# A graph layer's edge sort: one row per edge, or rows of 16 edges packed by one-hot products and written by adding scatters

## The reference

```python
def head(w1, bb1, w2, bb2, a1, aab1, a2, aab2):
    feats = jnp.maximum(x @ w1 + bb1, 0.0) @ w2 + bb2        # 256 -> 256 -> 64
    x_cat = jnp.concatenate([feats[row], feats[col], elem[:, None]], axis=1)
    hid = jnp.maximum(x_cat @ a1 + aab1, 0.0)
    e1 = (hid @ a2 + aab2)[:, 0]
    e1 = jax.nn.leaky_relu(e1, negative_slope=0.2)
    w = jnp.exp(e1 - jnp.max(e1))
    pooled = jax.ops.segment_sum(w[:, None] * feats[col], row, num_segments=n)
    row_sum = jax.ops.segment_sum(w, row, num_segments=n) + 1e-10
    return pooled / row_sum[:, None]
x = _layernorm(x + transpose(vmap(head)(...)).reshape(n, -1))
```

## Time and profile before

| | |
|---|---|
| time, median of 3 runs | 6067.9 us (6063.4 to 6071.91) |
| the profiled execution's own time | 6098.69 us |
| its span | 6096.9 us |
| PE / DVE / ACT / POOL busy in the span | 4346.8 / 4243.0 / 3138.2 / 3789.0 us |
| mean granted TensorE clock | 0.866 |
| instructions in the trace | 127641 |
| indirect DMAs of POOL | 1600 scatters, 1664 gathers |

### The profile page before, as it was taken

The page is one execution under the profiler, slowest core; times in us unless marked ns, Lnnn a source line. Parts: engine busy times, 40 slices in busy tenths (PEclk is TensorE's granted clock), DMA queues, the critical chain, the costliest instruction groups (busy, mean ns, idle before and its releaser), DMA issues.

```text
span 6096.9 us, 127641 instructions
## 1 busy us (share of the span) xinstructions
PE 4346.8 (71%) x24741; PEld 3053.9 (50%) x24742; DVE 4243.0 (70%) x23832; ACT 3138.2 (51%) x10707; POOL 3789.0 (62%) x3738
## 2 busy tenths in 40 slices
PE   3645555454555546189999999999999999999940
PEld 1423333332333323066667766676676766666630
DVE  7644444444444444378888888888888888888863
ACT  0211111111111111078888888888888888888842
POOL 6878777778777877745555555555555555555532
PEclk9867777776777777599999999999999999999975
DMA  1221222222122222267777777777777777777733
GB/s 59 50 47 29 50 33 43 38 39 46 30 50 32 44 36 36 50 202 217 217 218 216 218 216 216 216 218 215 216 216 218 218 218 212 213 219 216 210 114 119
DMA packets 298498, 833.67 MB, mean 137 GB/s; under 512 B 113010, under 2 KB 152050, under 8 KB 298342
## 3 DMA queue, kind: packets, MB, share of 16 engines
q0 software_dynamic: 184320, 666.30, 42.1%
q1 hardware_dynamic: 71614, 149.77, 8.0%
q10 hardware_dynamic: 42408, 16.21, 1.0%
HBM read 733.35 MB, written 96.91 MB: 136 GB/s over the span
## 4 chain that ended last, share of the span: by engine, by line
PE 36%; POOL 31%; issue 16%; ACT 6%; DMA 4%; DVE 4%; DVEq 0%; another core or an unknown queue 0%; SPq 0%; POOLq 0%; ACTq 0%
POOL records L556 31%; PE psum L753 15%; PE psum L740 9%; PE psum L757 9%; ACT z L850 4%; DMA out_dram<-z 3%; PE psum L766 2%; DVE z L1179 2%; DMA p_win<-p_table 1%; PE psum L777 1%; ACT onehot L879 1%; DVE acc L976 1%; ACT onehot_t L868 1%; DVE z L1169 1%; DVE acc L1228 1%
## 5 line engine op out<-in xcount | busy, mean ns | idle before, releaser
L587 POOL DMA_INDIRECT z<-qf_table,rec x1664 | 1598.1, 960 | 1565.9 <-PE psum L740 926.7
L556 POOL DMA_INDIRECT records<-z x1600 | 1942.5, 1214 | 503.5 <-issue 503.5
L850 ACT ACTIVATE z<-z 128x64 f32<-128x64 f32 x6656 | 1651.2, 335 | 56.7 <-ACT z L857 28.8
L753 PE MATMUL psum<-p_win,onehot_t 128*128 x9984 | 1438.0, 277 | 235.8 <-issue 128.0
L753 PEld LDWEIGHTS psum<-p_win,onehot_t 128*128 128x128 bf16 x9984 | 965.9, 97 | 805.3 <-issue 488.5
L740 PE MATMUL psum<-z,onehot 128*128 128x260 f32 x3328 | 1027.2, 391 | 2.6 <-DVE acc L1228 1.6
L757 PE MATMUL psum<-z,ident 128*128 128x258 f32 x3328 | 1006.6, 384 | 0.0
L1179 DVE SCALAR_TENSOR_TENSOR z<-z,a_b 128x129 f32<-128x129 f32 x3328 | 888.9, 290 | 0.0
L1179 DVE SCALAR_TENSOR_TENSOR z<-psum,a_b 128x129 f32<-128x129 f32 x3328 | 820.8, 282 | 3.3 <-issue 3.3
L651 PE MATMUL psum<-z,ones_b 125*128 125x400 bf16 (+1 forms) x1600 | 344.3, 310 | 656.2 <-DVE z L968 656.1
L1169 DVE TENSOR_TENSOR z<-z,psum 128x258 f32<-128x258 f32 x1664 | 690.3, 415 | 117.3 <-PE psum L757 87.0
(11 more groups left out here) (162 smaller groups left out, 5640.7 us busy)
## 6 DMA issues: line engine op xcount, KB each, us to landing
qf_table<-acc SPq DMA_DIRECT2D x100, 378.9 KB
p_table<-acc SPq DMA_DIRECT2D x100, 377.9 KB
p_win<-p_table SPq DMA_DIRECT2D x100, 377.9 KB
z<-qf_table,rec POOLq DMA_INDIRECT x1664
records<-z POOLq DMA_INDIRECT x1600
acc<-in_x_dram SPq DMA_DIRECT2D x25, 500.0 KB
z<-in_x_dram SPq DMA_DIRECT2D x20, 625.0 KB
out_dram<-z ACTq DMA_DIRECT2D x20, 625.0 KB
```

Source lines behind the costliest of these rows:

```text
L556: pool.indirect_dma_start(out=records, out_offset=bass.IndirectOffsetOnAxis(ap=pos_at[0:EP, s, c:c + 1], axis=0), in_=rec_out[0:EP, s, 4 * ...
L587: pool.indirect_dma_start(out=z_t[:, o + j, :], out_offset=None, in_=qf_table, in_offset=bass.IndirectOffsetOnAxis(ap=rec[:, o + j, 3:4].b ...
L753: mm = pe.matmul(to, onehot_t[:, j, :], p_flat[:, bass.ds((w % 2) * (3 * ZW) + (part * ZW + o), n)], start=(part == 0), stop=(part == 2 an ...
L850: op = act.activation(z_t[:, slot, o:o + DO], z_t[:, slot, o:o + DO], ACT.Copy, scale=z_t[:, slot, o + DO:o + HF])
```

## The change

A block is now 16 edge columns (100 blocks, four to a group, 2000 edges each). The 1600 scatters of single edges become three adding scatters per block:

- The place of each edge (`pick`) comes from PE as before, but the base of each column and window is worked out for the whole kernel in setup and added by PE, so that no count is carried from step to step. Setup therefore masks and keeps the histogram of each quarter of a block (`hist_take`), turns it around, sums it and makes three tables from it.
- A place is split in a chunk (16 records) and a slot in it (`split`). DVE makes `placed`, for each edge its six bfloat16 fields in its slot of 16 (`slots`), and the one-hot of the edge's chunk among 320 (`chunks`, 16 instructions per block). PE multiplies them (`place`, 16 products per block), which gives the sum of up to 320 chunk rows of 96 numbers; ACT takes it from PSUM (`take_sum`), PE turns it and fetches the block's step table (`turn_rows`), and DVE makes the row numbers (`row_ids`).
- POOL issues three indirect DMAs per block with `compute_op=ALU.add`, of 128, 128 and 64 rows of 384 bytes, into `sorted_rows`, which SP has filled with zeros. Before each block's three POOL waits until those of the block before have landed. That is 300 in all.
- The window one-hots move from DVE to ACT, with 16 Abs and 4 Relu instructions per block (`windows`). The features leave PSUM on ACT too, with the product with `A1` (`take_q`), and PE's transposes for them become 128 more columns of that product. ACT's work gets a written order like the others'.
- The loop has 26 turns of the group, since a block passes its last step three blocks after its first.
- Behind the loop, 13 bulk steps (`BULK`) read `sorted_rows` back (384 KB each), turn each field on PE, write the records' fields on DVE and ACT, and store them to `records`. DVE clears the accumulator before them, and they wait for all scatters.

Of the diff the core stands here; left out are the buffers' places, the semaphores, the arithmetic of the setup tables (some 45 more small DVE instructions, and four over 1600 columns before POOL's lines 536 to 540, which now come after the histogram), ACT's rewritten node work, which is as before, and the rewritten window arithmetic.

```diff
     EP = 125
     EC = E // EP
-    CPI = EC // GROUPS
-    SUBS = 4
-    LOT = CPI // SUBS
+    CB = 16
+    BLOCKS = EC // CB
     CH = 4
-    CHUNKS = LOT // CH
-    assert N == WN * W and E == EP * EC and CPI * GROUPS == EC and CHUNKS * CH * SUBS == CPI
+    PER = BLOCKS // GROUPS
+    S = 16
+    NF = 6
+    SF = S * NF
+    KC_MAX = 320
+    KB = [128, 128, 64]
+    assert N == WN * W and E == EP * EC and CB * BLOCKS == EC and PER * GROUPS == BLOCKS and CB == 4 * CH
...
+    CHUNKS = NT * P // S
+    sorted_rows = nc.dram_tensor("sorted_rows", (CHUNKS + 3 * P, SF), F32, kind="Internal").ap()
...
+        def sort_loop(eng, group):
+            group(0)
+            group(1)
+            with nc.Fori(2, GROUPS - 1, engines=bass.OrderedEngineSet([eng.engine]), hint_back_edge=True) as g:
+                group(g)
+            group(GROUPS - 1)
+            group(GROUPS)
...
-            for n in range(SUBS):
-                sp.wait_ge(s_scat[n], 16 * LOT * GROUPS)
+            sp.wait_ge(s_scat, 48 * BLOCKS)
             rec_d = records.rearrange("(p t) n -> p (t n)", p=P)
+            rows_g = sorted_rows[0:CHUNKS, :].rearrange("(g t c) n -> g t (c n)", t=P, c=P // S)
+            def load_stage(g):
+                since(sp, s_field_mm, g - 1)
+                sp.dma_start(stage[:, g % 2, :], rows_g[g, :, :]).then_inc(s_stage[g % 2], 16)
+            load_stage(0)
+            for g in range(BULK):
+                if g + 1 < BULK:
+                    load_stage(g + 1)
+                sp.wait_ge(s_field_a, g + 1)
+                sp.wait_ge(s_field_b, g + 1)
+                sp.dma_start(rec_d[:, g * P * 4:(g + 1) * P * 4], rec_all[:, g * P:(g + 1) * P, :].rearrange("p t n -> p (t n)")).then_inc(s_rec_st, 16)
+            sp.wait_ge(s_rec_st, 16 * BULK)
...
             def scatter(g):
-                for s in range(SUBS):
-                    pool.wait_ge(s_at, g * 2 * SUBS + 2 * s + 2)
-                    pool.sem_inc(s_passed, 1)
-                    for c in range(LOT):
-                        pool.indirect_dma_start(
-                            out=records, out_offset=bass.IndirectOffsetOnAxis(ap=pos_at[0:EP, s, c:c + 1], axis=0),
-                            in_=rec_out[0:EP, s, 4 * c:4 * c + 4], in_offset=None, compute_op=ALU.bypass).then_inc(s_scat[s], 16)
-            loop(pool, GROUPS, scatter)
+                for b in range(PER):
+                    if live_b(g, b, -3):
+                        h = g * PER + (b - 3)
+                        pool.wait_ge(s_row_i, h + 1)
+                        since(pool, s_scat, h * 48)
+                        pool.sem_inc(s_passed, 1)
+                        for k in range(3):
+                            pool.indirect_dma_start(
+                                out=sorted_rows, out_offset=bass.IndirectOffsetOnAxis(ap=row_i[0:KB[k], (b - 3) % 2, k:k + 1], axis=0),
+                                in_=rows_out[0:KB[k], (b - 3) % 2, 2 * (W + 1) + k * SF:2 * (W + 1) + (k + 1) * SF], in_offset=None, compute_op=ALU.add).then_inc(s_scat, 16)
+            sort_loop(pool, scatter)
+            pool.wait_ge(s_sum, 4 * BLOCKS)
+            pool.iota(win_iota, [[P, NT]], base=0, channel_multiplier=0, allow_small_or_imprecise_dtypes=True).then_inc(s_win_iota, 1)
...
             def prefix(g, q):
-                n = g * (CPI // CH) + q
+                n = g * (PER * 4) + q
                 pe.wait_ge(s_oh, n + 1)
-                since(pe, s_carry, n)
-                o = psum[:, q % 2, :]
-                for c in range(CH):
-                    oh = win_oh[0:EP, q % 2, c, :]
-                    pe.matmul(o[:, (c + 1) * W:(CH + 1) * W].rearrange("p (c w) -> p c w", w=W), ones_b[0:EP, :],
-                              oh.unsqueeze(1).to_broadcast([EP, CH - c, W]), start=(c == 0), stop=False, skip_group_check=True)
-                    mm = pe.matmul(o[:, c * W:(c + 1) * W], before[0:EP, :], oh, start=False, stop=(c == CH - 1),
-                                   skip_group_check=True)
-                mm.then_inc(s_count, 1)
+                since(pe, s_pos, n - 1)
+                o = psum[:, q % 2, 0:CH * W]
+                own = ident_b[0:BLOCKS, bass.ds(g * PER + q // 4, 1)].to_broadcast([BLOCKS, P])
+                at = slice(q % 4 * CH * W, (q % 4 + 1) * CH * W)
+                pe.matmul(o, own, base_hi[0:BLOCKS, at], start=True, stop=False)
+                pe.matmul(o, own, base_lo[0:BLOCKS, at], start=False, stop=False)
+                pe.matmul(o, before[0:EP, :], win_oh[0:EP, q // 4 % 2, q % 4 * CH:(q % 4 + 1) * CH, :].rearrange("p c w -> p (c w)"),
+                          start=False, stop=True).then_inc(s_count, 1)
+            def place(g, b, j):
+                n = (g * PER + (b - 2)) * 4 + j
+                pe.wait_ge(s_chunks, n + 1)
+                if j == 0:
+                    pe.wait_ge(s_placed, g * PER + (b - 1))
+                    since(pe, s_sum_ev, g * PER + (b - 2))
+                for c in range(j * CH, (j + 1) * CH):
+                    mm = pe.matmul(psum[0:SF, 7, 0:KC_MAX], placed[0:EP, b % 2, c, :], chunk_oh[0:EP, b % 2, c, :],
+                                   start=(c == 0), stop=(c == CB - 1))
+                mm.then_inc(s_sum, 1)
+            def turn_rows(g, b):
+                h = g * PER + (b - 3)
+                pe.wait_ge(s_sum_ev, h + 1)
+                since(pe, s_row_f, h)
+                since(pe, s_f_ev, min(g * 2 + b // 2 * 2, GROUPS * 2) if isinstance(g, int) else g * 2 + b // 2 * 2)
+                for k in range(3):
+                    pe.matmul(psum[0:KB[k], 4, 2 * (W + 1) + k * SF:2 * (W + 1) + (k + 1) * SF], chunk_t[0:SF, k * P:k * P + KB[k]], ident_b[0:SF, 0:SF], start=True, stop=True)
+                own = ident_b[0:BLOCKS, bass.ds(h, 1)].to_broadcast([BLOCKS, P])
+                for u in range(3):
+                    mm = pe.matmul(psum[:, 4, 0:2 * (W + 1)], own, step_p[0:BLOCKS, u, :], start=(u == 0), stop=(u == 2))
+                mm.then_inc(s_turned, 1)
...
+            pe.wait_ge(s_sum_ev, BLOCKS)
+            for g in range(BULK):
+                pe.wait_ge(s_stage[g % 2], g // 2 * 16 + 16)
+                since(pe, s_field_a, g - 1)
+                since(pe, s_field_b, g - 1)
+                for f in range(NF):
+                    mm = pe.matmul(psum[:, g % 2 * 6 + f // 3, f % 3 * P:(f % 3 + 1) * P],
+                                   stage[:, g % 2, :].rearrange("p (s f) -> p f s", f=NF)[:, f, :], ident[:, :], start=True, stop=True)
+                mm.then_inc(s_field_mm, 1)
...
+            def windows(g, b, j):
+                n = (g * PER + b) * 4 + j
+                since(act, s_pos, n - 7)
+                for c in range(j * CH, (j + 1) * CH):
+                    op = act.activation(win_oh[0:EP, b % 2, c, :], iota_win[0:EP, 0, :], ACT.Abs, scale=-1.0,
+                                        bias=edge_win[0:EP, bass.ds((g * PER + b) * CB + c, 1)])
+                op.then_inc(s_win_dist, 1)
+                act.wait_ge(s_win_dist, n + 1)
+                own = win_oh[0:EP, b % 2, j * CH:(j + 1) * CH, :].rearrange("p c w -> p (c w)")
+                act.activation(own, own, ACT.Relu, scale=-1.0, bias=ones_f[0:EP, 0:1]).then_inc(s_oh, 1)
+            def take_sum(g, b):
+                h = g * PER + (b - 3)
+                act.wait_ge(s_sum, h * 4 + 4)
+                since(act, s_turned, h)
+                act.activation(chunk_t[0:SF, :], psum[0:SF, 7, 0:KC_MAX], ACT.Copy).then_inc(s_sum_ev, 1)
...
+            def hist_take(n, b):
+                dve.wait_ge(s_hist, n + 1)
+                dve.tensor_tensor(hist_m[:, b, :, :, :], psum[:, b, 0:HG * HCOL * LO].rearrange("p (m c n) -> p m c n", m=HG, c=HCOL),
+                                  same_col.unsqueeze(1).to_broadcast([P, HG, HCOL, LO]), ALU.mult).then_inc(s_hist_mask, 1)
+                dve.wait_ge(s_hist_mask, n + 1)
+                dve.tensor_reduce(count_m[:, bass.ds(n * HG, HG), :], hist_m[:, b, :, :, :].rearrange("p m c n -> p m n c"), AX_X, ALU.add).then_inc(s_hist_ev, 1)
...
+            def pick(g, b, j):
+                n = (g * PER + b) * 4 + j
+                since(dve, s_pos, n)
+                dve.wait_ge(s_count, n + 1)
                 for c in range(CH):
+                    op = dve.scalar_tensor_tensor(out=picked[0:EP, c, :], in0=psum[0:EP, j % 2, c * W:(c + 1) * W], scalar=1.0,
+                                                  in1=win_oh[0:EP, b % 2, j * CH + c, :], op0=ALU.mult, op1=ALU.mult,
+                                                  accum_out=place_f[0:EP, b % 2, j * CH + c:j * CH + c + 1])
                 op.then_inc(s_pos, 1)
+            def split(g, b):
+                h, r = g * PER + (b - 1), (b - 1) % 2
+                dve.wait_ge(s_pos, h * 4 + 4)
+                dve.tensor_copy(place_i[0:EP, :], place_f[0:EP, r, :]).then_inc(s_split, 1)
+                dve.wait_ge(s_split, h * 4 + 1)
```

(66 more changed lines are left out.)

599 lines of the change are left out of this document (358 added, 241 removed).

## The result

The changed kernel takes **5817.0 us** (median of 4 runs, 5811.07 to 5817.94) where the kernel before took 6067.8 beside it: a ratio of **0.9585** (95% interval 0.9568 to 0.9601), 251 us less. The forecast was 5440 us with a range up to 5790. The direction was right, the gain 40% of the 628 us expected, and the time lies 27 us outside the range.

What follows compares the result with a forecast made beforehand. The prediction took POOL's issue of scatters to bound the first stage. Setup 185, loop 1625, drain 20, tail 115 and second stage 3522 gave a span of 5467 us; the median, 0.5% under the profiled run, was forecast at 5440, range 5230 to 5790.

Steps and rivals of the forecast that it cites:

- What bounds the kernel before: First stage: bound by POOL's issue of 1600 scatters, one every 1.52 us, 97 us per group; other engines have room.
- Loop: Sort loop: 65 us a group from three engines passing work over PSUM; 1625 us for 25 groups, plus 20 draining.
- DVE, PE, ACT per group: Sort loop: work per group of 56 us for DVE, 50 for PE at full clock, 48 for ACT.
- the prediction's 0.14 us: DVE's chunk one-hot by the skill's page, four bfloat16 columns at once; the sum would be lower by up to 150 us.
- Clock: PE in the sort loop: full clock, 2.4 GHz, since it is busy some three quarters with short pauses.
- Setup: Before the loop: loop start at 185 us, 57 later than in the kernel before.
- Tail: Behind the loop: 48.6 us of DVE work, 13 bulk steps in 61, and 5 for transfers; 115 us.
- Second stage: From the end of the sort to the end of the span: 3522 us, untouched by the change.
- (a): Sort loop: PE's clock stays low or handoffs bite harder; 79 us a group, 5790 us in all; chance 0.20.
- (b): Sort loop: engines overlap fully, a group costs DVE's 56 us; 5215 us in all; chance 0.12.
- (d): Sort loop: DVE keeps POOL from issuing scatters, a block takes 26.5 us; about 6750 us in all; chance 0.03.
- (e): Whole change: it doesn't do what it says, or row scatters cost POOL far more; about no change; chance 0.01.

Runs made afterwards that it cites:

- experiment 8: e1 with the scatters writing their rows without adding (records not whole, only the time read); 5526.3 us.
- experiment 7: e1 with DVE doing the nodes' work of each step before the four chunk one-hots; 5397.2 us.
- e1: Changed kernel with SP issuing the qf_table store before the p_table store; 5535.8 us, ratio 0.9073 to the kernel before.
- experiment 6: e1 with POOL splitting the weights beside the histogram and not behind it; the loop begins at 194.9 us, in e1 at 193.3.
- experiment 5: e1 with POOL clearing the accumulator beside the bulk steps and making win_iota before the last two blocks' scatters; 5460.4 us.
- e4: Changed kernel with DVE making each chunk one-hot twice, the extra one into a spare tile; 5945.5 us.
- series A: The follow-up runs from e1 to e4, on one chip; the kernel before took 6102.4 us there.
- series B: Follow-up runs on another chip, among them experiment 5, experiment 6 and experiment 7; the kernel before took 6065.8 us there.
- series C: Experiment 8 and e10, on another chip; the kernel before took 6093.3 us there.
- e10: e1 plus the changes of experiment 5 and experiment 7, with every 125-row load and store cut in 112 and 13; 5280.1 us, ratio 0.8665.

## Why the prediction was wrong, and where it was right

- **What bounds the kernel before**: right. The scatters left the chain and were hidden by a wide margin (experiment 8).
- **Loop: the failed step.** The forecast priced the work of the engines and their handoffs over PSUM: the sum of each step's longest, 69, less slack, 65 us. It had no term for the landing of the stores that ACT now waits for. The change moved window one-hots and features to ACT, behind `take_q`, whose wait had cost little as long as the loop waited for POOL anyway. The missing term is a wait of 16.7 us a group (418.2 us in 25), of which 12.7 are paid. With the wait gone, in three different ways, a group costs 66.6 to 67.6. One resource was left out: a buffer that a store gives back. That 65 and 66.6 lie so close is in part luck: DVE's work was put some 5 us a group too high, and 4 us a group were the order that experiment 7 changes, for which the sum had no term.
- **DVE, PE, ACT per group.** Forecast 56, 50 and 48 us. From the window of e1 (busy share times 66.6): DVE 1106.08 / 1450 gives 50.8, PE 54.7 at a clock of 0.93, ACT 43.6. ACT's 43.6 is 4 below its forecast, PE's 5 above at the lower clock. The chunk one-hot was forecast at 0.24; in the kernel after four take 0.85 us from the first's start to the next instruction's (1041.86 to 1042.71), so 0.21 each. Three comparisons with one number per partition of its trace, by their duration in ns, two on float32 and then the one-hot:

```profile
L1572 DVE TENSOR_SCALAR z<-z x2: 267/268/270, 5587.1 to 5587.3; 104x100 f32<-104x100 f32 x2
L1389 DVE TENSOR_SCALAR acc<-acc,z x1: 1086/1086/1086, 2219.4 to 2219.4; 100x1664 bf16<-100x1664 f32 x1
L1320 DVE TENSOR_SCALAR acc<-z x1600: 284/299/618, 217.3 to 2192.8; 125x320 bf16<-125x320 bf16 x178
```

The two float32 ones lie 1564 columns and 818 ns apart, 0.52 ns a column on a fixed 216 ns. At that rate 320 columns would last 383 ns. The one-hot lasts 299, which is the same 216 and 0.26 a column, twice the rate. The Trainium skill ("VectorE: DVE Perf Modes", "The perf-mode tier table") has four columns at once for bfloat16 against two; by that rule, the trace agrees. What was too low in the prediction's 0.14 us is the fixed part: the rate came true, the price did not. Two slips in the working change nothing: ACT's parts for the one-hots, the sum and the waits add up to 31 and not 32, and DVE's lower bound to 50 and not 49.

- **Clock.** Full clock was forecast; it was 0.86 from 400 to 1900, with pauses that were not short. It rose with every wait that went: from 400 to 1700 it is 0.93 in e1 and 0.96 in e7, with PE's work unchanged. That it only follows the waits is the simplest reading; how much of the gains it gave back was not separated.
- **Setup**: 193.7 and not 185. The histogram took 102 us (41.3 to 143.4) and not 85, 2.04 us per step: 0.94 for the one-hots, as forecast, 0.59 for masking with the wait for it, and 0.52 for reducing, where 0.75 was forecast for both and their waits. Against that, the edge arithmetic ended 7 us sooner, and POOL's parts took 25 us and not 32: their price of 6.5 each had been read from instructions that took turns with DVE's one-hots (experiment 6).
- **Tail**: 115 forecast, 115.6 measured. That is luck: DVE's work was 10 us longer and the bulk steps were 8 us shorter (experiment 5).
- **Second stage**: 34 us shorter than in the profile before, with the same code. The experiments show that this is not the change. It took 3531, 3525, 3529 and 3528 us in e1 to e4 (series A), 3485, 3491 and 3487 in e5 to e7 (series B) and 3522 in e8 (series C), all with the same second stage; the profiled execution before stood 0.5% above its median, and is of the longer kind. The gain read before the second stage, 2575.1 - 2321.7 = 253 us, is that of the timed runs, 251.
- **Rivals.** (a) named 79 us per group and 5790 us, and that is the number that came: but by a low clock or one-hots at 0.39 us, neither of which is the cause. The number was right for a wrong reason. (b) is out: e10's loop still takes 62 us ((1794.8 - 253.2) / 99 blocks, by four). (d): the turns are real (experiment 6) but hit DVE in setup, not POOL's issues in the loop (1.55 us, at most 2.10). (e) is out: a scatter of rows cost POOL 1.55 us, hidden. The range failed because no case in it held a transfer that ends a wait on ACT.

The rows of e10 for the last point:

```profile
L659 POOL DMA_INDIRECT sorted_rows<-z x300: 1426/1555/2654, 253.2 to 1794.8; - x150
...
200.00:1750.00 1550.00, 1320.10 (x5500) 748.99 (x5500) 1277.53 (x6575) 1083.52 (x2768) 442.25 (x288) 0.96 0.29 64
```

DVE is busy 82% there: what is left is near the work of the busiest engine. What bounds the last 11 us above DVE's 51 stays open.

## What to carry to other kernels

When a bound is taken away, list every wait of every engine in the loop, stores that give buffers back first: a wait that was free behind the old bound may be next, and what the written order puts behind it waits too. A queue should issue first what is ready first. And where a transfer's row count has no large divisor up to 16, look at its DMA share: 125 rows ran at a third of it, here and in a norm that the change had not touched.

## What the runs showed of the hardware

- Transfers of 125 rows ran at a share of 0.27 to 0.34, cut in 112 and 13 at 0.90 to 0.94 (stores of the loop, and the norm).
- An adding scatter of 128 rows of 384 bytes took POOL 1.55 us to issue and landed in 3.3 (2.8 to 12.0); without adding the issue took 0.96 us, less than the 1.19 of the old scatter of 125 rows of 16 bytes.
- A DVE instruction of two SBUF sources beside POOL's casts waited for their end: up to 5.3 us for one that takes 0.4 to 0.7. The masking, with one source in PSUM, took its usual 0.41 beside the same cast (51.27 in experiment 6).
- The same second stage is 1.2% longer in series A than in B; a term of a sum that is taken from one profiled execution should be compared within a series.
